# Folding the term rows of two batch groups further on GpSimd, so that TensorE sums fewer of them

## The reference

```python
kv = jnp.einsum('bhil,bhjl->bijhl', k_, v_)
y = irfft(rfft(kv, n=512) * rfft(ssm_kernel, n=512))[..., :256]
out = y + kv * D[None, None, None, :, None]
out = jnp.einsum('bijhl,bhil->bjhl', out, q_)      # a sum over 8 channels i
x = x + tanh(g_xattn[0]) * out
x = x + tanh(g_ffn[0]) * moe(layernorm(x))
```

## Time and profile before

| | us |
|---|---|
| median of 3 runs (lowest to highest) | 230.38 (230.21 to 231.25) |
| time of the profiled execution | 231.63 |
| its span from the first to the last instruction | 229.8 |
| TensorE busy | 199.0 (87% of the span) |
| VectorE busy | 149.5 (65%) |
| GpSimd busy | 125.3 (55%) |
| ScalarE busy | 81.0 (35%) |
| the transposes and sums of `turn_r` (L1070), 192 matmuls | 23.1 |
| the folds (L596), 16 instructions | 20.3 |

### The profile page before, as it was taken

The page is one execution under the profiler, slowest core; times in us unless marked ns, Lnnn a source line. Parts: engine busy times, 40 slices in busy tenths (PEclk is TensorE's granted clock), DMA queues, the critical chain, the costliest instruction groups (busy, mean ns, idle before and its releaser), DMA issues.

```text
span 229.8 us, 3951 instructions
## 1 busy us (share of the span) xinstructions
PE 199.0 (87%) x1344; PEld 179.8 (78%) x1344; DVE 149.5 (65%) x483; ACT 81.0 (35%) x153; POOL 125.3 (55%) x129
## 2 busy tenths in 40 slices
PE   0276999978999799999999899898679999999970
PEld 0254879856998699898998898797579999999960
DVE  5749678599788987589665853643357655676330
ACT  2421521535542561233243164340243454234200
POOL 3596856177755689415850261080071875777652
PEclk9999799999999999999999999999999999999995
DMA  4789992000000020020500996878812798522221
GB/s 110 264 227 350 379 405 114 0 0 4 3 3 0 19 73 3 0 93 3 183 0 32 316 290 207 267 200 282 247 55 70 261 308 246 174 80 83 66 85 46
DMA packets 24101, 31.87 MB, mean 139 GB/s; under 512 B 3390, under 2 KB 21574, under 8 KB 24080
## 3 DMA queue, kind: packets, MB, share of 16 engines
q1 hardware_dynamic: 21424, 24.75, 33.7%
q0 software_dynamic: 2304, 6.05, 8.0%
q10 hardware_dynamic: 352, 0.81, 1.0%
HBM read 21.32 MB, written 10.54 MB: 139 GB/s over the span
## 4 chain that ended last, share of the span: by engine, by line
PE 71%; DMA 10%; DVE 6%; issue 6%; ACT 2%; POOL 2%; POOLq 1%; ACTq 0%; DVEq 0%; SPq 0%
PE fb L1131 14%; PE z L1045 11%; PE z L1131 11%; PE tp L1070 10%; PE z L1155 8%; PE z L1042 6%; PE fb L1155 6%; DMA kskip_scratch<-kp 3%; DMA xd_scratch<-xrow,dest 3%; DVE terms L441 3%; DMA toep<-kskip_scratch 2%; PE tp L1166 1%; DMA dcol<-skip_d 1%; DMA kv<-xd_scratch 1%; PE tp L1080 1%
## 5 line engine op out<-in xcount | busy, mean ns | idle before, releaser
L441 DVE TENSOR_TENSOR terms<-z,qr 128x512 f32<-128x512 f32 (+2 forms) x192 | 48.8, 325 | 11.5 <-PE z L1045 11.2
L1045 PE MATMUL z<-kv,toep 128*128 128x288 f32 x128 | 43.1, 419 | 0.0
L422 POOL TENSOR_TENSOR kv<-ct 128x768 f32<-128x768 f32 x15 | 28.3, 1884 | 16.4 <-PE z L1045 14.6
L1042 PEld LDWEIGHTS z<-kv,toep 128*128 128x128 f32 x128 | 23.0, 197 | 14.7 <-issue 9.5
L1131 PE MATMUL fb<-xTh,wh_gu 128*128 128x256 f32 (+1 forms) x104 | 32.5, 312 | 1.7 <-issue 1.7
L1042 PE MATMUL z<-kv,toep 128*128 128x144 f32 x128 | 28.0, 302 | 6.6 <-DVE terms L441 4.9
L644 POOL DMA_INDIRECT kv<-base_scratch,tok x16 | 22.2, 1390 | 16.2 <-DMA base_scratch<-x_sb 10.8
L1131 PE MATMUL fb<-xTl,wh_gu 128*128 128x256 f32 (+1 forms) x104 | 29.0, 279 | 0.0
L1131 PE MATMUL fb<-xTh,wl_gu 128*128 128x256 f32 (+1 forms) x104 | 29.0, 279 | 0.0
L596 POOL TENSOR_TENSOR terms<-terms 128x512 f32<-128x512 f32 x16 | 20.3, 1284 | 12.7 <-DVE terms L441 12.7
L1131 PE MATMUL z<-xTh,wh_gu 128*128 128x256 f32 (+1 forms) x88 | 26.0, 295 | 1.2 <-DVE xTl L938 1.2
(11 more groups left out here) (122 smaller groups left out, 375.9 us busy)
## 6 DMA issues: line engine op xcount, KB each, us to landing
terms<-w SPq DMA_DIRECT2D x16, 352.0 KB, 4.8
ct<-ctxt SPq DMA_DIRECT2D x3, 768.0 KB, 7.3
xd_scratch<-xrow SPq DMA_DIRECT2D x4, 516.0 KB, 9.5
kv<-xd_scratch SPq DMA_DIRECT2D x8, 258.0 KB
out<-x_sb SPq DMA_DIRECT2D x8, 256.0 KB
base_scratch<-x_sb SPq DMA_DIRECT2D x8, 256.0 KB
terms<-w SPq DMA_DIRECT2D x8, 256.0 KB, 5.8
x_sb<-x SPq DMA_DIRECT2D x3, 512.0 KB, 6.3
```

The costliest lines, as they stand in the source:

```text
L422: eng.tensor_tensor(dst, left, right, ALU.mult)
L441: return eng.tensor_tensor(view(terms, t0 + row * TROW + col, [[64, 2], *td]), view(src, zo, [[512, 2], *zd]), view(qr, q0 + qo, [[CW, 2], ...
L1042: pe.matmul(view(z[s % 2], k * 512 + GB, [[PL, NPL], [1, GB]]), toep[:, h, P:2 * P], view(kv, o, [[PL, NPL], [1, GB]]), start=True, stop=F ...
L1045: mm = pe.matmul(z[s % 2][:, k, 0:KVH], toep[:, h, 0:P], view(kv, o, [[1, KVH]]), start=False, stop=True, skip_group_check=True)
```

## The change

Group 2 is folded in two steps, from 8 rows to 4 and from 4 to 2, and TensorE adds 2 rows. Group 3 is folded in three steps, to a single row, and TensorE only transposes it. Each step is an instruction of its own: 128x512, 128x256 and, in group 3, 128x128 elements, and a step waits for the end of the one before it. Only the last step raises `folded`. Where the folds stand in GpSimd's list, and where `turn_r` stands in TensorE's, is as before.

```diff
 FULL_TERMS = 2
+FOLDS = (0, 0, 2, 3)
 def terms_of(g):
-    return TERMS if g < FULL_TERMS else TERMS // 2
+    return TERMS >> FOLDS[g]
             def fold(s):
                 g, u = unit(s)
                 pool.wait_ge(prods, s + 1)
-                low, high = (view(terms, first_head(g, u) * 64 + i * 4 * TROW, [[TROW, 4], [1, 128]])
-                             for i in range(2))
-                pool.tensor_tensor(low, low, high, ALU.add).then_inc(folded, 1)
+                for n in range(FOLDS[g]):
+                    half = TERMS >> n + 1
+                    low, high = (view(terms, first_head(g, u) * 64 + i * half * TROW, [[TROW, half], [1, 128]])
+                                 for i in range(2))
+                    ins = pool.tensor_tensor(low, low, high, ALU.add)
+                    if n < FOLDS[g] - 1:
+                        chain(ins)
+                ins.then_inc(folded, 1)
```

## The result

The changed kernel takes 238.47 us (median of 4 runs, 238.18 to 238.75). The kernel before, timed beside it, has a median of 230.67. The ratio is 1.0297 with a 95% interval from 1.0246 to 1.0348: slower by 3%. The forecast was 236.8 in a range from 233.3 to 239.4. The profiled execution took 238.56 with a span of 236.8; the span of before was 229.8, so 7.0 us of the difference can be read from the two traces.

A forecast was written before the change was run, and what follows sets the result against it. TensorE has 71% of the chain, and GpSimd's folds behind two scatters end just ahead of `turn_r`. Longer folds, 8.7, less 4.9 give 3.8; clock falls add 2.6: +6.4 us, median 236.8, range 233.3 to 239.4.

The forecast's parts named there:

- The gain on TensorE: Both `turn_r` steps of groups 2 and 3 drop 8 and 12 transposes each: 4.65 us off the chain.
- The folds: On GpSimd, a fold takes 2.06 us in group 2 (+0.81) and 2.62 in group 3 (+1.37); bounds 0.55/0.82 and 0.95/1.65.
- Group 2: Folds behind the scatter of group 0 end at 94.3; `turn_r` starts 3.0 us later, TensorE idling.
- Group 3: Four folds behind the scatter of group 1 end at 125.2; `turn_r` starts 5.8 us later, TensorE idling 4.7.
- I let VectorE make up 0.5 of it: VectorE recovers 0.5 of the 2.1 us delay before group 1's scatter, which then moves by 1.6 us.
- The clock: TensorE's clock falls at each of the two new idle times, 1.3 us each (between 0 and 1.7), 2.6 together.
- The shift ahead of the clock: Longer folds, 8.7 us, less 4.9 for gains, slack and VectorE waits: 3.8 us, carried to the end.
- Rival (e): A later wait, a landing of the last scatter, absorbs 1 to 2 us: 232 to 233 us; chance 0.05.
- (a): No fall of TensorE's clock, or one within the idle time: +3.8, 234.2 us; chance 0.20.
- (b): Links between fold steps cost 0.24 us and both clock falls come in full: +8.9, 239.3 us; chance 0.12.
- (c): Small folds cost only their elements, no clock fall to speak of: +0.6, 231.0 us; chance 0.06.
- (d): GpSimd has room, folds are ready when TensorE comes: 3.9 us faster, 226.5 us; chance 0.07.

The follow-up runs named there:

- the gain alone: Changed kernel without the folds' second and third steps, so sums of groups 2 and 3 lack terms: 226.55 us, ratio 0.9803 to the kernel before.
- the filling: Changed kernel plus 20 and 38 unread identity transposes on TensorE before the waits of groups 2 and 3: 235.46 us, ratio 1.0189 to the kernel before.
- group 2 alone: Kernel before with only group 2 folded to two rows, group 3 keeping its single fold: 234.68 us, ratio 1.0118.

## Why the prediction was right, and where its sizes were off

**The gain on TensorE** was put at 4.65 us, less 0.75 at the places step, 3.9. The run with the gain alone measured 4.05.

**The folds** were priced at 0.73 and 0.46 us for the new shapes and 0.10 for a link. They took 0.736 and 0.459, and a dependent step started 0.07 to 0.08 after the one before it. Four pairs took 10.40 us where 10.48 had been forecast (4 x 2.62). The two bounds, 0.24 a link and no fixed cost at all, were both far off.

**Group 2.** `turn_r` was to start at +3.0; its matmuls start at 94.54 where they started at 91.42, +3.1, of which 0.3 stood ahead of all folds. **Group 3** was to start at +5.8 without the clock and at +7.1 with the first fall. It starts at 127.11 where it started at 119.53, +7.6. Without those 0.3 us it is +7.3, that is 5.8 and the 1.5 that the first fall cost (below). The step "I let VectorE make up 0.5 of it" was near: VectorE came out of the logits at +3.85 (101.99 against 98.14) and ended the gate at +3.5, so it made up 0.3.

**The clock** is the term that was mis-sized. The forecast put 1.3 us on each fall. Its price can be read by holding the two places of the changed kernel against the same places of the run with the filling, where the clock was 1.00. From `turn_r` of group 2 to the end of the convolutions behind it the changed kernel takes 4.16 us (94.54 to 98.70) and the filled one 2.62 (93.94 to 96.56): 1.5. From `turn_r` of group 3 to the end of the 12 matmuls behind it they take 5.65 and 3.32: 2.3. Together that is 3.9 where 2.6 stood. Even the "full" price of 1.7 was too low for the second, since the lower clock held on through more than 4 us of busy work. The reason given for a low price, that a slow stretch would lie partly in the wait, did not help: in the second wait the clock stood at 0.50 from 125.25 on, 1.9 us ahead of the release, and the slow stretch behind it was still the longer of the two; at the first it fell only as the wait ended (0.99 from 92.30 to 94.50).

**The shift ahead of the clock**, forecast at 3.8, was right. At the places step of group 2 the two traces are 8.1 us apart (135.77 against 127.67), and 8.1 at the last scatter as well (157.10 against 149.00). Less 0.3 from the start and 3.9 for the clock that is 3.9. The run with the filling shows it alone: its last scatter starts at 152.94 where that of before started at 149.00, +3.9, or +4.2 counted from where the two stood at 56 us (56.05 against 56.31).

**At the end** the two traces come closer again: the rows are read for the experts at 166.27 in place of 159.08, +7.2, since that read follows 5.3 us behind the last scatter in place of 6.2, and the first expert starts at +7.0. Rival (e) named such a landing. But the distance from the last scatter to that read lies between 5.3 and 6.5 us in the traces of all the runs here, 5.4 in the run of the gain alone, so that the change shortened it is not shown.

So the mechanism and its place were right. By the rows the clock was 1.3 us too cheap and nearly everything else stood as forecast. The whole time is a coarser judge. The medians moved by 7.8 where 6.4 was forecast, the profiled executions by 6.9, and the ratio of 1.0297, with its interval, says 5.7 to 8.0. That 6.9 lies so near to 6.4 is in part luck: the clock cost 1.3 more, and the end of that one execution gave 1 us back. By the same medians the filling gave back 3.0 of the 7.8 us and left 4.9. Read so, the clock was near its 2.6 and the waiting cost more than its 3.8; the intervals of the two runs are too wide to choose between that and the rows.

**The rivals.** (a), no fall of the clock, fell with the rows at 0.50 and with the filled run. Its argument was not empty, as the wait of 2.16 us without a fall and the fastest execution of group 2 alone show. (b), 239.3, came nearer to the measured 238.5 than the forecast did, but for the wrong reason: the links were cheap, only the falls were dear. (c) and (d) fell with the measured folds. That GpSimd had "room" was true on average and in the wrong places: it still idled 7.1 us ahead of first fold steps in the kernel after, while TensorE waited for it twice.

The rule of the Trainium skill (TensorE: Matmul & The Clock Gate, "What's actually happening"), that idleness throttles the array and activity releases it, is borne out by both falls and by the run in which useless transposes prevented them. Which wait is followed by a fall is not shown here: one of 2.41 us was, one of 2.16 us in the same trace was not.

## What to carry to other kernels

When work goes to an engine that looks half idle, read its list at the moment when the result is due: what stands in front of that work, and how long it is busy without a gap, decides, not its share of the span. Price a wait of TensorE with the clock that it may cost behind it; here that was two fifths to a half of the loss, 3.0 of 7.8 us by the medians and 3.9 of 7.8 by the rows. The change was not wrong in itself: with two DMA-issuing steps moved out of the way, the same folding takes 1.3% less time than before (1.4% with group 3 folded to two rows). With the same two steps moved to a place where the folds lie beside the small operations of VectorE on which TensorE waits, it gave nothing.

## What was not expected of the hardware

Beside GpSimd's two-input additions, some operations of VectorE take many times their length, and others none: the comparison of 128x32 elements 1.09 us in place of 0.18, four additions of 128x8 elements 2.52 in place of 0.77. The products of VectorE, which read one input from PSUM, took 1.54 us for a pair of heads with and without a fold beside them.

The traces show when it happens. In the run with scatters in slots 24 and 32 and two rows in both groups, GpSimd's fold and VectorE's operations stand so:

```profile
97.54 1.27 POOL L600 TENSOR_TENSOR terms<-terms 128x512 f32<-128x512 f32 x1
```

```profile
97.76 1.08 DVE L863 TENSOR_SCALAR eq<-sh 128x32 f32<-128x32 f32 x1
98.88 0.19 DVE L865 TENSOR_TENSOR t<-eq,prio 128x32 f32<-128x32 f32 x1
```

The comparison starts while the fold runs and ends 0.03 us behind it. The multiplication behind it falls into the gap ahead of the next step, which starts at 98.89, and keeps its 0.19 us. The multiplication is not spared as such: in the full change with the same scatters it starts inside a fold (99.37, the fold from 99.25 to 100.52) and takes 1.20 us.

Between 59 and 135 us the thirteen traces hold 74 operations of VectorE that took more than 0.05 us over their shortest time; 72 of them end 0.02 to 0.05 us behind the end of a fold step. All are operations with two inputs from SBUF, or the kind that takes a tensor and a scalar. Operations that read PSUM, reductions and the statistics of the normalisation ran inside folds at their usual length. GpSimd's indirect DMA issues had little of this effect: beside them the comparison took 0.24 and 0.34 us, the other two of the 74. But one of the 72 had started during such an issue, 0.56 us ahead of the fold that it outlasted (the additions of 2.52 us), and another, the comparison of 1.55 us, had started in the step ahead of the one that it outlasted.
